# Four graph layers on one core: whole double rows stored by the first dense stage, no clearing of half rows in the first edge stage

## The reference, cut to what matters

```python
# x: 100000 nodes x 128 floats; src, dst: 50000 edges, sorted by dst
h = relu(layernorm(x));  x = x + L0(h)      # degree-normalised sums over edges, then a dense layer, relu, residual
h = relu(layernorm(x));  x = x + L1(h)      # per edge: relu(h[src] @ W[type] + b), summed at dst
h = relu(layernorm(x));  x = x + L2(h)      # two normalised convolutions and a decoder
h = relu(layernorm(x));  x = x + L3(h)      # attention over edges, softmax per dst

def L0(x, edge_index, W, b):                # loops: every node is its own neighbour too
    norm = dis[row] * dis[col]
    agg = segment_sum(x[col] * norm[:, None], row)
    return x + relu(agg @ W.T + b)
```

## Time and profile before

| | |
|---|---|
| time, median of 3 runs | 7372.24 us (7370.35 to 7379.27) |
| profiled execution, its own time | 7381.27 us |
| its span, first to last instruction | 7379.6 us |
| busy: PE, DVE, ACT, POOL | 47%, 69%, 39%, 68% |
| share of 16 DMA engines: q1, q0 | 43.7%, 18.0% |
| first edge stage, indexed adds of L543, first to last start | 874.9 to 1618.6 us |
| first dense stage, stores of L986, first to last start | 1646.9 to 2185.9 us |

### The profile page before, as it was taken

How to read it: one execution, slowest core, us unless ns; L and a number is a source line. 1 busy time by engine, 2 the same in 40 slices (tenths; PEclk the granted TensorE clock), 3 DMA queues, 4 the chain that set the end, 5 groups by cost and what they waited for, 6 DMA issues and landing times. The chain is left out here.

```text
span 7379.6 us, 112554 instructions
## 1 busy us (share of the span) xinstructions
PE 3468.4 (47%) x18041; PEld 2586.3 (35%) x18041; DVE 5061.2 (69%) x19573; ACT 2846.2 (39%) x7222; POOL 5036.6 (68%) x4720
## 2 busy tenths in 40 slices
PE   7655366656658777740027766000885233333000
PEld 1111255545656666630015555000664122222000
DVE  7999587877878888877767776422774355555554
ACT  0366211127763333336656665000331255554222
POOL 0377788874447777777767772776788677776677
PEclk9766699988889999975558888555998555555555
DMA  7488587769984444447779998222996333333443
GB/s 292 152 289 286 164 145 140 139 135 287 286 237 118 117 116 119 116 128 209 207 252 362 371 354 271 62 52 67 341 337 209 93 103 102 103 103 91 126 136 114
DMA packets 1197152, 1352.42 MB, mean 183 GB/s; under 512 B 234425, under 2 KB 997419, under 8 KB 1186568
## 3 DMA queue, kind: packets, MB, share of 16 engines
q1 hardware_dynamic: 990310, 1028.66, 43.7%
q0 software_dynamic: 206768, 323.00, 18.0%
HBM read 731.99 MB, written 646.74 MB: 187 GB/s over the span
## 5 line engine op out<-in xcount | busy, mean ns | idle before, releaser
L702 POOL DMA_INDIRECT dense<-t_xs,ends x784 | 786.3, 1003 | 266.9 <-issue 215.6
L1842 PE MATMUL ps<-dense,w 128*128 128x256 f32 x3136 | 736.0, 388 | 215.6 <-DVE dense L1518 214.7
L543 POOL DMA_INDIRECT t_src<-tot,sidx x392 | 614.9, 1569 | 138.2 <-issue 93.9
L1842 PEld LDWEIGHTS ps<-dense,w 128*128 128x128 f32 x3136 | 585.0, 191 | 333.5 <-DVE dense L1518 219.3
L1768 PE MATMUL ps<-oneh_c,oneh_p 128*128 128x395 f16 x1568 | 457.7, 429 | 279.6 <-DVE oneh_c L879 271.4
L702 POOL DMA_INDIRECT dense<-t_y,ends x392 | 384.0, 980 | 259.5 <-DVE ends L1622 170.8
L1518 DVE SCALAR_TENSOR_TENSOR dense<-dense,xT 128x256 f32<-128x256 f32 x1568 | 546.6, 419 | 6.4 <-ACT xT L2022 2.8
L677 POOL DMA_INDIRECT t_yacc<-dense,gq x392 | 453.5, 1157 | 129.9 <-issue 109.7
L640 POOL DMA_INDIRECT out_rows<-dense,sidx x392 | 387.4, 988 | 183.0 <-issue 112.5
L640 POOL DMA_INDIRECT t_xs<-dense,sidx x392 | 399.0, 1018 | 122.7 <-issue 78.6
L1209 POOL DMA_INDIRECT dense<-out_rows,ends x392 | 387.4, 988 | 121.4 <-issue 121.1
(11 more groups left out here) (331 smaller groups left out, 11912.8 us busy)
## 6 DMA issues: line engine op xcount, KB each, us to landing
dense<-t_xs SPq DMA_DIRECT2D x78, 1320.0 KB
dense<-in_x SPq DMA_DIRECT2D x156, 640.0 KB
t_xs<-dense SPq DMA_DIRECT2D x98, 528.0 KB
t_xs<-hb SPq DMA_DIRECT2D x78, 660.0 KB, 6.3
t_src<-dense SPq DMA_DIRECT2D x99, 512.0 KB
t_sum<-dense SPq DMA_DIRECT2D x98, 512.0 KB, 4.0
t_src<-dense SPq DMA_DIRECT2D x78, 640.0 KB, 3.3
dense<-t_src SPq DMA_DIRECT2D x78, 640.0 KB
```

The lines of the kernel that those rows point to most:

```text
L543: gp.indirect_dma_start(t_src, bass.IndirectOffsetOnAxis(ap=sidx[:, p.k, c:c + 1], axis=0), tot[:, p.k, c, :], None, compute_op=ALU.add).t ...
L702: gp.indirect_dma_start(rows[:, p.k, c, :], None, table, bass.IndirectOffsetOnAxis(ap=gidx[:, p.k, c:c + 1], axis=0)) \
L1842: i = nc.tensor.matmul(ps[:, o:o + 2 * P], w1[:, k, :], xm[:, p.w, k, :], start=(k == 0), stop=(k == R - 1))
```

## The change

The clearing of the left half rows in the first edge stage is removed, and with it the wait at its end. In the first dense stage VectorE and ScalarE write their results into the right half of 264-float rows (`x1o`, in `pairs0`), whose left half is zero, and SyncE stores the whole double rows. Two of the three `pairs0` tiles lie in `dense` (areas 6 to 10), the third in the memory of `hb`, which becomes a view of one tile. At the start of the dense stage GpSimd zeros all three (2640 floats a partition each), and SyncE, ScalarE and VectorE wait for it before their loops. The bias result, in `oa` before, is written in place.

```diff
-        hb = [sb(f"hb{i}", [P, K, XW1]) for i in range(3)]
+        spare_rows = sb("spare_rows", [P, 3 * K * XW1])
+        hb = [spare_rows[:, i * K * XW1:(i + 1) * K * XW1].rearrange("p (k f) -> p k f", k=K) for i in range(3)]
...
+        pairs0 = [t.rearrange("p (k f) -> p k f", k=K) for t in
+                  (dense[:, 6 * KD:6 * KD + K * W2], dense[:, 6 * KD + K * W2:6 * KD + 2 * K * W2], spare_rows[:, 0:K * W2])]
+        x1o = [t[:, :, XW1:XW1 + D] for t in pairs0]
...
-            def clear_sums(p):
-                if p.u % 2 == 0:
-                    sp.dma_start(t_xs[bass.ds((p.r * UNROLL + p.u) * (CW // 2), CW), 0:XW1].rearrange("(p k) f -> p k f", k=8),
-                                 zrow).then_inc(S0["clear"].sem, 16)
...
-            pair_loop(sp, (rest_of_rows, 0), (clear_sums, 0))
-            sp.wait_ge(S0["clear"].sem, S0["clear"].after(16 * NCLEAR))
+            pair_loop(sp, (rest_of_rows, 0))
...
-                sp.dma_start(t_xs[bass.ds(b * BR, p * K), XW1:2 * XW1].rearrange("(p k) f -> p k f", k=K), hb[u][0:p]) \
+                sp.dma_start(rows_of(t_xs, b, p), pairs0[u][0:p]) \
                     .then_inc(L0["sto"][u].sem, 16)
+            sp.wait_ge(ZH["zeroed"].sem, ZH["zeroed"].after(1))
...
-            for t in hb:
-                gp.memset(t[:, :, D:XW1], 0.0)
...
+            for t in pairs0:
+                i = gp.memset(t, 0.0)
+            i.then_inc(ZH["zeroed"].sem, 1)
...
-                    i = nc.vector.scalar_tensor_tensor(out=oa[u][0:p, k, :], in0=ps[0:p, ZC + k * P:ZC + (k + 1) * P],
+                    i = nc.vector.scalar_tensor_tensor(out=x1o[u][0:p, k, :], in0=ps[0:p, ZC + k * P:ZC + (k + 1) * P],
...
-                nc.vector.scalar_tensor_tensor(out=hb[u][0:p, :, 0:D], in0=oa[u][0:p], scalar=0.0, in1=ob_h[u][0:p],
+                nc.vector.scalar_tensor_tensor(out=x1o[u][0:p], in0=x1o[u][0:p], scalar=0.0, in1=ob_h[u][0:p],
...
+            v.wait_ge(ZH["zeroed"].sem, ZH["zeroed"].after(1))
             node_loop(v, (conv0_rest, 1))
...
-                nc.scalar.activation(hb[u][0:p, :, D], dis[1][0:p, bass.ds(b * K, K)], ACT.Copy).then_inc(L0["nm"].sem, 1)
+                nc.scalar.activation(pairs0[u][0:p, :, XW1 + D], dis[1][0:p, bass.ds(b * K, K)], ACT.Copy).then_inc(L0["nm"].sem, 1)
...
+            a.wait_ge(ZH["zeroed"].sem, ZH["zeroed"].after(1))
             node_loop(a, (conv0_first, 0))
```

More of the change, by code:

```diff
@@ L384, in gnn @@
         x2 = [t[:, :, XW1:XW1 + D] for t in xs]
+        pairs0 = [t.rearrange("p (k f) -> p k f", k=K) for t in
+                  (dense[:, 6 * KD:6 * KD + K * W2], dense[:, 6 * KD + K * W2:6 * KD + 2 * K * W2], spare_rows[:, 0:K * W2])]
+        x1o = [t[:, :, XW1:XW1 + D] for t in pairs0]
+        assert 6 * KD + 2 * K * W2 <= 12 * KD
         h2 = [t[:, :, 0:D] for t in xs]
@@ L459, in slots @@
             return [n * len(range(u, NB + 1, SLOTS)) for u in range(SLOTS)]
-        S0 = phase("setup", 1, "ld lde ldk zrow clear zero pad made calc deg hot mm root")
+        S0 = phase("setup", 1, "ld lde ldk zrow zero pad made calc deg hot mm root")
         LN = "copy bn mv var std rs sc "
@@ L476, in gnn @@
                    {"ld": slots(16), "lda": slots(16), "sto": slots(16)})
+        ZH = phase("halves", 1, "zeroed")
         E1 = phase("edge", NPAIR, "ring bn mv std rs nb h tx txc masked xw relu back", GP)
```

## The result

The changed kernel took 7379.0 us in the median of 20 runs, the kernel before 7369.6 in 20 runs beside them. The medians are 9.4 us apart. The ratio is 1.0015, with a 95% interval of 1.0008 to 1.0022, so +11 us (6 to 16). In a second set, 12 runs of it against 35 of the kernel before gave 1.0000 (0.9989 to 1.0011). Its two profiled executions took 7371.9 and 7391.5 us; those of the kernel before took 7381.3 and 7380.6. Executions of one kernel differ by 30 us and more, so the reasons have to be read from stages, and each stage from several profiles.

The account below looks back on a forecast made before the run. GpSimd's own pace was taken to bound the first edge stage, DMA throughput the first dense stage. Terms -14 + 7 + 30 + 1 = +24 us gave 7396 us, with an 8-in-10 range of 7352 to 7428.

Parts of the forecast that it names:

- No change: Whole kernel: measured time between 7357.5 and 7387 us, within 0.2% of before; chance 0.30.
- Clears gone: First edge stage: without the clears' transfers, 367 of GpSimd's indexed adds each get 0.037 us faster, -14 us.
- Memsets: Start of the first dense stage: three memsets of 2.3 us delay all loads and nothing hides them, +7 us.
- Old store: First dense stage: storing half rows in 1280 packets of 528 bytes takes 2.80 us, at the clears' 35 ns each.
- new store: First dense stage: storing 1.352 MB of double rows takes 3.33 us at the zeroing's 406 GB/s.
- The step: First dense stage: each step grows by 0.38 us from the larger store, +30 us over 79 blocks, bounds -10 and +54.
- with no owner: First dense stage: 0.66 us of a step's 6.69 us of queue time, left after loads (3.23) and old store (2.80).
- rival B: First dense stage: turnaround goes with the small packets, a step grows 0.1 us, +8 in all, 7374 us; chance 0.21.
- 0.53 us: First dense stage: a step's growth from 2.80 to 3.33 us of store, before unused queue time absorbs some.
- The rest of the dense stage: First dense stage: VectorE's wider row pitch costs nothing, covered by 1.2 us of slack a step; last store +1 us.

## Why the prediction was right and wrong, point by point

The forecast was +24 us, slower by over 0.2%. Measured were +11 in the first set and 0 in the second: inside the range of 7352 to 7428, on the forecast's side or level, and under the 14.7 us from which I had called it slower. "No change", which had 0.30, is what happened. The measured time lies inside the range, but not by the forecast's reasons: its largest term, +30, wasn't there, and the stages add up to -5. That +11 in one set lies on the forecast's side is luck, as far as the runs show.

- *Clears gone, -14.* Right in place and cause, a little small: 14.0 us between the two first profiles, 16 over all. The flat 1.856 us an add behind the last clear was the row to go by.
- *Memsets, +7.* Right: 7.4 us, nothing over them. What the step missed is how cheap it was to hide them. VectorE stands idle for 18.6 us at the end of the stage before, as the first line behind the gate shows above.
- *Old store, 2.80 us, new store 3.33.* The old one fits: 1280 packets are 2.6 us at the price of the clears alone and 2.88 in the mix. The new one wasn't priced alone; beside loads at 406 GB/s it takes no more than 6.90 - 3.23 = 3.67.
- *The step, +0.38 us, +30 in all.* This is the term that was mis-sized: it measured 0.0 (6.91 to 6.90 in the means). The step that failed stands before it, in what bounds the kernel: "the stage is bound by DMA throughput". The packets held the engines for 96.9% of the time, but that share counts how long packets are under way, not what the engines could move: it reached 112.1% with two stores. At the measured prices the loads and the old store need 3.23 + 2.6 to 2.9, so 5.8 to 6.1 us of a step of 6.91. The other 0.8 to 1.1 us took in the whole growth of the store. The 3.23 us for loads is an estimate, from the rate of a store of zeros. With no store the loads kept the engines busy for 0.604 x 5.95 = 3.6 us a step. By that the old kernel had 0.4 to 0.7 us of room, and the changed one none. I had seen 0.66 us "with no owner" and gave them to rival B, at 0.21; the forecast let only 0.15 of the 0.53 us go under. The Trainium skill's figure of about 358 GB/s for one core, half of what it gives for a stack of HBM (DMA: Bandwidth & Descriptors, Specifications), would have put the step at 7.44 us. The changed kernel moves 381 GB/s in this stage, so the trace doesn't agree.

Five kernels in order of DMA work show it best. Loads at 406 GB/s and the store at its price (estimates), then the share of the DMA engines and the step as measured:

| store | DMA work, us | share | step, us |
|---|---|---|---|
| none | 3.23 | 60.4% | 5.95 |
| half rows side by side, 5280 bytes | 3.23 + 1.67 | 86.5% | 6.46 |
| half rows, 528 bytes (before) | 3.23 + 2.6 to 2.9 | 96.9% | 6.91 |
| double rows, 10560 bytes (after) | 3.23 + 3.33 | 97.1% | 6.90 |
| double row in two stores, 528 bytes | 3.23 + 5.8 | 112.1% | 9.00 |

Up to some 6 us of work, the step grows by a third to a half of what the DMA engines get more to do, and from there to 6.56 not at all. The last line, whose work is taken from its own step, shows no room by construction. Waits between load, compute and store, and VectorE's meetings with GpSimd, set the first lines together with the DMA engines. This is argued from the table, not shown, and which chain of them it is isn't settled. A kernel with more buffers a tile would tell; none was run.

- *The rest of the dense stage.* No cost showed, as forecast. But the 5.67 us of VectorE's "work" in a step hold about 1.5 us of waiting for GpSimd (2.96 us for an operation that takes 1.49 alone), so the slack of compute was read too small.
- *What lies behind the stage* was taken as untouched, and isn't quite. The third edge stage gathers whole double rows with indexed DMAs. Their group from 3254 to 3748 us in the kernel before and from 3250 to 3748 us in the changed one:

```profile
L702 POOL DMA_INDIRECT dense<-t_xs,ends x387 | 375.5, 970 | 124.8 <-issue 97.8 <-ACT ends L2038 27.0
```

```profile
L708 POOL DMA_INDIRECT dense<-t_xs,ends x387 | 380.0, 982 | 124.6 <-issue 92.0 <-ACT ends L2044 32.6
```

An issue takes 982 ns and not 970. In five profiles with the old form of the dense stage the mean is 960 to 974 ns, in nine with the new form 975 to 982, and the stage takes 519.9 to 525.1 us and 525.0 to 527.9, 4 us more in the mean. The cause isn't known: these instructions, their tiles and the rows that they read are the same in both sources, and it is so with clears put back, with two stores and with the table zeroed in setup.

The stages of the profiles add up to -16 + 7 + 0 + 4 = -5 us. The times say +11 and 0. The gap of 5 to 16 us stays open. From its first load to the stage behind it the last dense stage takes 653 to 678 us, with no edit near it, and two profiles of the changed kernel (661 and 674) can't show a shift of 10. In the three profiles with the memsets on VectorE it takes 653 to 655 us, in the eleven others 661 or more. The cause isn't known, and a part of what that version gains may lie there.

## What to carry to other kernels

A DMA share near 1 isn't a throughput limit until the bytes at the best rate seen, plus the small packets at their own price, fill the step: price the work first, and what is missing from the step is room for a larger transfer. Here a share of 97% left room for 660 KB more a step, and two other kernels showed 105% and 112%. Taking transfers out of a stage that another engine paces gives only what its waits lose to them (16 us for 98 transfers of 2.08 us, 204 us in all), so it is the place where transfers cost least. Before paying for their removal elsewhere, hide the set-up on an engine that waits at the stage's end. Where executions differ by 30 us, forecast and read stages, and take several profiles of each.

## What the runs showed of the hardware that wasn't expected

Stores of rows with gaps between them ran at 260 GB/s in packets of 528 bytes (the clears alone in setup). In the mix they are estimated at 235 GB/s in packets of 528 and 251 in packets of 1056, with the loads taken at 406. The 4096-byte packets of the zeroing ran at 406. The Trainium skill (DMA: Bandwidth & Descriptors, Specifications) puts 512 bytes as the least size for line rate; neither 528 nor 1056 bytes reached it in these runs. Whether the gaps and the rows' alignment or the size of the packet is behind it wasn't separated.

The share of the DMA engines in the profile passed 100% in two kernels (105.4% and 112.1%).

VectorE's operation on 128x1280 floats took 1.49 us alone. Started while GpSimd's addition of the same size ran, it ended about 1.35 us after that one in all such cases of the stretches read (up to 4.24 us long; mean 2.96). Where VectorE had started first it took 1.49 us, and it was GpSimd's addition that grew (up to 4.22 us from 2.90).
